# Two attention layers: the key tile packed to four heads on 32-row slots, with 32-row score matmuls

## The reference, cut to what matters

```python
def _L0_attn_ref(x, wq, wk, wv, wo, bo):
    q = split_heads(x @ wq)            # (b, 16 heads, t, 8)
    k = split_heads(x @ wk)
    v = split_heads(x @ wv)
    scores = jnp.einsum('bhqd,bhkd->bhqk', q, k)
    scores = jnp.where(causal, scores, -jnp.inf)
    attn = jax.nn.softmax(scores / np.sqrt(HEAD_DIM), axis=-1)
    ctx = jnp.einsum('bhqk,bhkd->bhqd', attn, v)
    return ctx.transpose(0, 2, 1, 3).reshape(b, t, D) @ wo + bo
```

## Time and profile before

| | us |
|---|---|
| median of 3 runs | 1316.02 (1314.12 to 1316.12) |
| span of the profiled execution | 1311.0 |
| PE busy | 1194.1 (91%) |
| DVE busy | 1044.4 (80%) |
| ACT busy | 723.5 (55%) |
| mean granted clock of TensorE | 0.975 of full speed |

### The profile page before, as it was taken

How to read it: one execution, slowest core, us unless ns; L and a number is a source line. 1 busy time by engine, 2 the same in 40 slices (tenths; PEclk the granted TensorE clock), 3 DMA queues, 4 the chain that set the end, 5 groups by cost and what they waited for, 6 DMA issues and landing times.

```text
span 1311.0 us, 21446 instructions
## 1 busy us (share of the span) xinstructions
PE 1194.1 (91%) x7781; PEld 510.1 (39%) x7781; DVE 1044.4 (80%) x3015; ACT 723.5 (55%) x861; POOL 66.6 (5%) x64
## 2 busy tenths in 40 slices
PE   1999958999999999999699979599999999999997
PEld 1455533333333333334455537233333333333336
DVE  8976588999999887875447567799999989878764
ACT  1322115566777777777332224156667777777773
POOL 5111010000000000000101000100000000000000
PEclk9999979999999999999799989799999999999999
DMA  4100142000000000000000000510000000000001
GB/s 147 34 1 1 39 131 58 2 1 2 2 1 1 2 1 2 1 1 2 1 0 1 1 1 25 154 48 2 2 1 2 2 1 1 2 1 2 2 2 33
DMA packets 23510, 23.26 MB, mean 18 GB/s; under 512 B 3134, under 2 KB 21220, under 8 KB 23404
## 3 DMA queue, kind: packets, MB, share of 16 engines
q1 hardware_dynamic: 22252, 18.73, 4.9%
q0 software_dynamic: 1152, 3.15, 0.9%
HBM read 13.20 MB, written 8.39 MB: 16 GB/s over the span
## 4 chain that ended last, share of the span: by engine, by line
PE 70%; DVE 22%; issue 4%; ACT 2%; DMA 1%; SPq 0%; DVEq 0%; ACTq 0%
PE psum L1184 18%; PE psum L1204 17%; PE psum L1164 14%; PE psum L442 9%; DVE part_max L1314 8%; PE psum L466 2%; PE psum L903 2%; PE psum L1171 2%; DVE junk L1320 2%; DVE xn L167 1%; DVE norm_v L150 1%; PE psum L1224 1%; PE psum L918 1%; DVE norm_stats L141 1%; PE psum L427 1%
## 5 line engine op out<-in xcount | busy, mean ns | idle before, releaser
L1275 ACT ACTIVATE hidden<-psum,exp_scale 128x1024 f32<-128x1024 f32 (+3 forms) x640 | 597.7, 984 | 258.9 <-PE psum L1164 137.3
L1314 DVE TENSOR_REDUCE part_max<-psum 128x1 f32<-128x512 f32 x768 | 492.1, 686 | 59.1 <-PE psum L1204 53.9
L1204 PE MATMUL psum<-k_slots,q_slots 128*128 128x512 f16 (+3 forms) x1280 | 401.2, 356 | 34.2 <-DVE part_max L1314 12.2
L1164 PE MATMUL psum<-q_slots,k_slots 128*128 128x512 f16 (+3 forms) x1280 | 330.9, 348 | 6.3 <-ACT hidden L1275 3.5
L1184 PE MATMUL psum<-hidden,v_aug 128*9 128x512 f32 (+3 forms) x2560 | 293.7, 531 | 0.1
L1320 DVE CUSTOM_DVE_ANT_0 junk<-psum,causal_add 128x384 bf16<-128x384 f32 (+3 forms) x512 | 230.6, 488 | 49.0 <-PE psum L1204 45.9
L1204 PEld LDWEIGHTS psum<-k_slots,q_slots 128*128 128x128 f16 x1280 | 114.5, 97 | 361.1 <-DVE part_max L1314 177.5
L442 PE MATMUL psum<-parts,w_parts 128*128 128x512 f16 x768 | 180.4, 387 | 1.9 <-DVE parts L843 1.9
L1164 PEld LDWEIGHTS psum<-q_slots,k_slots 128*128 128x128 f16 x1280 | 118.3, 98 | 97.8 <-ACT hidden L1275 13.9
L442 PEld LDWEIGHTS psum<-parts,w_parts 128*128 128x128 f16 x768 | 73.7, 99 | 83.1 <-issue 6.8
L586 ACT CAST parts<-psum 128x512 f16<-128x512 f32 x64 | 37.2, 588 | 107.2 <-PE psum L427 107.2
(11 more groups left out here) (170 smaller groups left out, 730.5 us busy)
## 6 DMA issues: line engine op xcount, KB each, us to landing
q_slots<-q_rows SPq DMA_DIRECT2D x8, 512.0 KB, 3.7
k_slots<-k_rows POOLq DMA_DIRECT2D x24, 128.0 KB, 4.1
q_rows<-parts SPq DMA_DIRECT2D x18, 128.0 KB, 2.7
k_rows<-parts SPq DMA_DIRECT2D x18, 128.0 KB, 2.4
q_slots<-in_L_ffn_W_dram SPq DMA_DIRECT2D x2, 1024.0 KB, 6.5
k_slots<-k_rows SPq DMA_DIRECT2D x8, 128.0 KB, 3.9
q_slots<-nm_parts SPq DMA_DIRECT2D x64, 4.0 KB
out_dram<-x_res SPq DMA_DIRECT2D x4, 256.0 KB, 2.3
```

Of the source, the lines that this page charges most:

```text
L1164: last = pe.matmul(psum[:, S_BANKS + 2 * (tile % 2) + par, off:CH], k_slots[:, G * g + 2 * pr + par, j * P:(j + 1) * P], q_slots[:, g, c * ...
L1204: last = pe.matmul(psum[:, bank, 0:w], q_slots[:, g, qb * P:(qb + 1) * P], k_slots[:, G * g + h, kc * CH:kc * CH + w], start=True, stop=True)
L1275: act.activation(probs[:, tile % NP, :, off:CH], psum[:, bank:bank + 2, off:CH], ACT.Exp, scale=exp_scale[:, layer:layer + 1]).then_inc(ex ...
L1314: dve.tensor_reduce(dst, psum[:, bank, :], axis=AX.X, op=ALU.max).then_inc(ring_read, 1)
```

## The change

`k_slots` becomes [128, 4 groups, 2048], laid out as `q_slots` is: the four heads of a group share a plane, each on its own 32 partitions, and nothing is padded. Each score matmul and each max-unit matmul takes the 32 partitions of its head from both operands, so the array is addressed as a 32x128 tile that depends on the head (rows 0, 32, 64 or 96). Mask matmuls and transposes stay at 128x128, the values matmuls as they were. The memset of zeros covers one plane, and the second memset no longer waits for it. One DMA loads the keys of a chunk for all four heads; the number of bytes is the same.

```diff
-        k_slots = sb("k_slots", [P, H, T], F16)
+        k_slots = sb("k_slots", [P, NG, T], F16)
...
-                    pool.memset(k_slots[:, :, :].rearrange("p h t -> p (h t)").bitcast(I32), 0).then_inc(slots_set, 1)
-                    pool.wait_ge(slots_set, 1)
+                    pool.memset(k_slots[:, 1, :].bitcast(I32), 0).then_inc(slots_set, 1)
                     pool.memset(k_slots[0:H * MAX_PARTS, 0, :], MAX_UNIT).then_inc(slots_set, 1)
...
-            def load_k_rows(engine, n, h):
+            def load_rows(engine, slots, m, n):
 
                 cols = slice(n * CH, (n + 1) * CH)
-                return engine.dma_start(k_slots[SLOT * h:SLOT * (h + 1), h::G, cols],
-                                        slot_dram[1].rearrange("(g h) i d t -> h (i d) g t", h=G)[h, :, :, cols])
+                return engine.dma_start(slots[:, :, cols],
+                                        slot_dram[m].rearrange("(g h) i d t -> (h i d) g t", h=G)[:, :, cols])
+
+            def rows_of(h):
+                return slice(SLOT * h, SLOT * (h + 1))
...
                     for par in range(2):
+                        rows = rows_of(2 * pr + par)
                         last = pe.matmul(psum[:, S_BANKS + 2 * (tile % 2) + par, off:CH],
-                                         k_slots[:, G * g + 2 * pr + par, j * P:(j + 1) * P],
-                                         q_slots[:, g, c * CH + off:(c + 1) * CH],
+                                         k_slots[rows, g, j * P:(j + 1) * P],
+                                         q_slots[rows, g, c * CH + off:(c + 1) * CH],
                                          start=True, stop=q not in diagonal)
...
-                        last = pe.matmul(psum[:, bank, 0:w], q_slots[:, g, qb * P:(qb + 1) * P],
-                                         k_slots[:, G * g + h, kc * CH:kc * CH + w], start=True, stop=True)
+                        last = pe.matmul(psum[:, bank, 0:w], q_slots[rows_of(h), g, qb * P:(qb + 1) * P],
+                                         k_slots[rows_of(h), g, kc * CH:kc * CH + w], start=True, stop=True)
...
-                    for h in range(G):
-                        load_k_rows(pool, proj.order[n], h).then_inc(k_landed[proj.order[n] - 1], 16)
+                    load_rows(pool, k_slots, 1, proj.order[n]).then_inc(k_landed[proj.order[n] - 1], 16)
...
                     if n == 0:
-                        for h in range(G):
-                            load_k_rows(sp, c, h).then_inc(q_landed[c], 16)
+                        load_rows(sp, k_slots, 1, c).then_inc(q_landed[c], 16)
```

## The result

The changed kernel is slower: 1385.19 us, median of four runs, against 1315.89 us, a ratio of 1.0498 with the interval 1.0442 to 1.0555. Its runs spread from 1370.28 to 1412.91 us, and they go with the mean granted clock of TensorE: 0.840 in the shortest, 0.827 and 0.82 in the two between, 0.799 in the longest; before had 0.975 in its profiled run and 0.968 or more in every later one. The longest is the one that was profiled, with a span of 1410.6 us, so its lines show the fall at its largest.

The account below looks back on a forecast made before the run. The prediction took PE to bound the kernel, with DVE and ACT near behind. Its terms, -12.5 - 1.4 - 52 + 16 = -50 us, took the span from 1311 to 1261 and the time from 1316 to 1266 us; range 1232 to 1302.

Parts of the forecast that it names:

- Start, -12.5: Program start: the shorter POOL memset frees DVE's norm_v and moves the whole program, -12.5 us, bounds -13 and -9.
- The 5 us between span and time: Whole program: the median of the runs was put 5 us above the profiled span, 1261 to 1266 us.
- Key load, -1.4: Second attention's wait for keys: one DMA issue instead of four, -1.4 us, bounds -2 and +1.
- Overlap: Score pairs in ordinary turns: matmuls on different rows overlap, 0.27 us a pair instead of 0.43, saving 0.32 a turn.
- Rival B: Slower, mainly diagonal turns: no overlap of row tiles, 612 new changes of shape cost PE time, 1347 us; chance 0.10.
- DVE as the next bound: Ordinary four-unit turns: PE falls from 2.81 to 2.3 to 2.5 us, below or at DVE's 2.39.
- the sum's 9 us: First attention, 350 to 480 us: of DVE's 12.1 us idle, 9 counted as given back.
- Diagonal turns, +16: Diagonal turns: 512 changes of shape around masks and transposes, net +41 us of PE, 40% on the path, +16 us.
- the price of a change: PE, wherever the matmul shape changes: about 0.10 to 0.11 us each, read from units and values in the trace.
- Ordinary turns, -52: Scores and units in ordinary turns: idle time given back, 26 us per attention, 52 in both.
- rival C: Attention's ordinary turns: PE's clock falls to 1.2 GHz, 1.5 us more a turn, about 1640 us; chance 0.05.

Follow-up runs that it names:

- the filler: Changed kernel with two extra 128-row, 512-column matmuls on constant weights behind each turn's values: 1458.84 us.
- both kernels of the grouped order: Kernel before, shortened start, turn reordered to both score tiles, masks, all units, values: 1331.13 us with 32-row scores, 1442.39 us with 128 rows everywhere.
- one row group: Changed kernel with every score and unit matmul on partitions 0 to 31, so nothing overlaps (computation left wrong): 1873.59 us.
- the kernel with 64 rows: Kernel before with the shortened start, score and unit matmuls on 64 rows, their head's 32 and 32 zeros: 1346.49 us.
- The split order with full rows: Kernel before, shortened start, 128 rows everywhere, turn reordered to score tiles, masks, half the units, values, other half: 1311.28 us.
- the start alone: Kernel before with the first memset cut to one plane, other planes zeroed later by DMA copies, matmuls at 128 rows: 1301.34 us.

## Why the prediction was wrong, step by step

- **Start, -12.5: right.** 12.5 measured by itself.
- **The 5 us between span and time: misread.** A run's time lies about 2 us above its own span (1412.91 and 1410.6; 1312.87 and 1311.0); the 5 came from setting the span of one execution against the median of others. It does not touch the error here.
- **Key load, -1.4: mis-sized.** I took 3.9 us for the 512 KB load, since the query load of that size lands in 3.7; it lands in 4.9 (SP) and 5.1 (POOL, 4.1 before). 1.0 of the 1.4 us is lost again, and PE's wait at the second attention fell by 0.46 us, from 5.13 to 4.67: inside the bounds that I gave.
- **Overlap: right, and fuller than I took.** 0.27 a pair was the value taken; the second matmul starts at most 0.01 us behind the first, not 0.055, so a pair costs 0.215. Rival B's "doesn't overlap" is out. The Trainium skill, "TensorE: Matmul & The Clock Gate", "Measured speedup vs the span model", has 3.07x for four row tiles; here a unit, a pair and a unit, four narrow matmuls, start within 0.01 us, by the trace's modelled times.
- **DVE as the next bound: right.** Turn 2.47 us against 2.39 worked out, with PE waiting for `part_max`. At full clock the step of 43.0 us became 40.5, 2.5 where the sum's 9 us for 130 us of that stage make 3.
- **Diagonal turns, +16: the price of a change is right, the net can't be read off.** c is 0.105 to 0.11 in turns with two and with six changes, and 0.11 at the masks. What the 512 changes cost on the path isn't separated from the clock, as many diagonal turns lie in half-clock stretches.
- **Ordinary turns, -52: this is the term that failed, by way of rival C.** It took a clock of 1.00 for granted, the level of the earlier trace rows. The gain is there at full clock only; where 26 us were to be saved per attention, the profiled run lost 34 in the first and 55 in the second. C had the mechanism, "a quarter of the array's rows in use" (beside it stood that PE would wait more, which alone gives 0.93 to 0.97, not 0.50), and was given 0.05 with no more reason than "No row shows narrow tiles alone". That is a reason not to know, not a reason to think it unlikely: I had weighed it by the earlier trace rows, where PE was idle, and taken from 2.96 busy us of 4 at 1.00 that a busy PE keeps its clock. Those matmuls had full rows. No row of before could separate a busy PE from a full array, and I should have kept the whole cost of C in the range, whose upper end of 1302 held none of it.
- **C's size was wrong too.** I had 4.6 us for a turn of four units at 1.2 GHz; it takes 3.74, as the overlap holds there too. And I had the clock down in all ordinary turns (1640 us); it was down in a part of them, so the runs end at 1370 to 1413.
- In my expectations I missed the times of seven kernels, though not what each was to decide about the clock. With scores narrow alone I left out that units between the pairs change shape as well; with units narrow alone the same, once more. With the filler and both kernels of the grouped order I left out that DVE needs its units spread over the turn: the ring holds three. With one row group I had the clock too high (0.75 to 0.85). Why the kernel with 64 rows took 1346 us where I had 1265 to 1285, at about the clock that I had, was not taken apart. The split order with full rows, which I had as neutral, came out 10 us above the start alone.

## What to carry to other kernels

Before matmuls are cut to fewer rows, look at which other full-row work stands in the same stretch: here the scores could go to 32 rows and keep the clock at 0.96, and both passes could not. The zeros in the padded planes were not wasted in this respect. Count the changes of shape in a turn, 0.105 to 0.11 us each, against 0.215 us for each 512-column matmul that gets hidden, and put matmuls of a shape in one group only as far as the engine that reads them stays fed. And read the clock line before anything else: at half clock PE's busy share looks as good as ever.

## What the runs showed of the hardware

- TensorE's granted clock fell with the rows that score and unit matmuls used, not with PE's busy time: PE was 129.97 of 130 us busy at 0.50 with both on 32 rows, and 104.6 of 130 us busy at 0.97 with both on 128, of which 96 held zeros in the key tile. Values of 32 columns instead of nine left it at 0.799 to 0.840.
- Matmuls on different 32-row groups start within 0.01 us. A change of shape costs 0.105 to 0.11 us in either direction, and as much at half clock: behind the values two units take 0.96 us, behind a score pair 0.85. The Trainium skill, "TensorEngine Tiling (Array Packing)", "Key Properties", says that a change of mode drains TensorE; the trace agrees, and puts this price on it.
- A memset of POOL held a DVE instruction on four elements for 11.64 us; the memset cut, it takes 0.71. DVE's batch-norm statistics, ahead of it, ran while the long memset was going on.
- One DMA of 512 KB for 128 partitions took 4.9 us from issue to landing (SP, median of two), each of four of 128 KB for 32 partitions 3.9.
